# Gated feed-forward: activations in two float32r parts, weights cast to float32r in place, where activations had three bf16 parts

## The chip, the cores and the metric

One core of a Trainium2 chip runs the whole kernel. The metric is the device time of one execution in microseconds, lower is better. The engines are TensorE (PE, its weight loads apart as PEld), VectorE (DVE), ScalarE (ACT), GpSimd (POOL) and the queue of SyncE (SP), each with its own order of instructions, held together by semaphores.

## The reference

The kernel is a two-layer decoder over 8 batches of 256 tokens and 256 features, with six sublayers, each followed by a residual sum and a layer norm. The change touches the last one:

```python
wg = w_gate.astype(f32) / 127          # 768 x 256, integers from -127 to 127
wu = w_up.astype(f32) / 127            # 768 x 256
wd = w_down.astype(f32) / 127          # 256 x 768
gate = einsum('bsd,hd->bsh', x, wg)
up = einsum('bsd,hd->bsh', x, wu)
h = silu(gate) * up
x = layernorm(x + einsum('bsh,dh->bsd', h, wd))
```

Activations are float32. The weights are small integers, and so one narrow part holds each of them without loss.

## The kernel before

The sublayer before the feed-forward is a masked cross-attention over 8 batches (`attention_mask`, L1343). Its last rounds and the feed-forward overlap: on every engine the order is written out by hand.

**Tiling.** The feed-forward works on pairs of batches (PAIR = 512 token columns). A pair has HT = 6 chunks of 128 hidden features, and there are NG = 24 chunks n. `gate_up(n)` (L1473) multiplies, for each of gate and up, two blocks k of 128 features by the 512 columns, three parts each: 6 matmuls into one bank for gate (L1481 to L1488) and 6 for up. The banks alternate with n: the gate half of chunk n waits for `prod` of chunk n-2, the up half for `h_made` of n-2 (L1483). `down(t)` (L1500) makes the output of batch t: for each of 2 token tiles 6 blocks k of hidden features and 3 parts, 36 matmuls of 256 columns. There the stationary tile is a 128x128 slice of an activation part, and the moving one is `w_down`. It waits for all six `low` of its pair.

**Parts.** A float32 activation is held as three bf16 parts. For x, `split_x` (L1945, GpSimd) makes them per batch in four instructions: high copy, remainder, middle copy, low difference. Batches 0 to 4 are split during the attention (L1984), 5 to 7 between the first `low` (L1994 to L1999). For the hidden values the parts are `high` (ScalarE, L1715), `rest` (VectorE, remainder, L1834), `middle` (ScalarE, L1721) and `low` (GpSimd, L1962).

**A chunk's way.** `tanh(n)` (ScalarE, reads the gate bank), `hidden(n)` (VectorE, L1820: first half `(tanh+1)*gate`, which signals `prod`; second half times up, which signals `h_made`), `high`, `rest`, `middle`, `low`. ScalarE's order is tanh(n), middle(n-1), high(n) (L1733 to L1742), VectorE's rest(n-1), hidden(n) (L1879 to L1881). VectorE also takes the normalisation of the outputs in between: `out_begin` (L1840) after hidden of the chunks n with n % 6 of 3 and 4, `out_end` (L1867) after 5 and 0. The last batch of the attention is normalised after hidden(5) (L1887) and, on GpSimd, after low(4) (L1992, `normalise`).

**TensorE's order at the end of the attention.** gate_up(0) stands in the last round (L1579); gate_up(1) to (7) stand between the last transposes, products and projection (L1600 to L1619); from gate_up(8) on, `down` of the pair before stands behind the chunks with n % 6 of 2 and 3 (L1620 to L1628); the last two batches' products end the program (L1629 to L1643).

**Memory.** The integer weights are loaded into `dist` (L3078) and cast by `cast_weights` (L1937, GpSimd) to bf16 in `rw`. The x parts lie in `dist`, the hidden parts in `w_all_mats`, `c_feat`, `dist` and `bnd` (L1373 to L1381).

## Time and profile before

| | us |
|---|---|
| median of 3 runs | 887.89 |
| runs | 886.81 to 888.18 |
| span of the profiled execution (first to last instruction) | 885.5 |
| what lies around the span (median less span) | 2.4 |
| TensorE matmul busy in it | 847.8 (96%) |
| VectorE busy | 680.2 (77%) |
| ScalarE busy | 618.7 (70%) |
| GpSimd busy | 417.6 (47%) |

The profile gives the span of one execution; its time is that and a start and an end around it, which the 2.4 us stand for. A busy engine is one whose instructions run; a matmul's recorded length holds its way through the array too, so that the pace of matmuls is read from their starts. Times of the rows are microseconds from the span's start.

### The profile page before, as it was taken

Reading aid. Unit: us, or ns where it says so; the run is one execution under the profiler, and the core shown is the slowest. Engines: PE = TensorE matmul, PEld = TensorE weight load, DVE = VectorE, ACT = ScalarE, POOL = GpSimd, SP = SyncE. Lnnn points to the kernel's source line nnn. Section 1 sums busy time; section 2 is a strip of 40 time slices with the busy share of each in tenths; the row PEclk is TensorE's granted clock in tenths of the full one; section 3 lists DMA queues with packets and bytes.
Section 4 is the critical chain, followed back from the end, with each engine's and each line's share of the span. In section 5 each row is a group of like instructions: output and inputs, shape, how many; then the busy total and the mean of one; then the engine's idle time right before and its main releaser. Section 6 shows DMA issues by size and latency. Waiting matters only on the chain.

```text
span 885.5 us, 21124 instructions
## 1 busy us (share of the span) xinstructions
PE 847.8 (96%) x7018; PEld 613.6 (69%) x7029; DVE 680.2 (77%) x2504; ACT 618.7 (70%) x1605; POOL 417.6 (47%) x447
## 2 busy tenths in 40 slices
PE   9998999999989989999999999999999999999996
PEld 7876777777768667777676766767666766746554
DVE  4988798888997767787686766838888888866876
ACT  4547877777872578787787777748888888854441
POOL 1256546775451345435455342245445555346532
PEclk9999999999999999999999999999999999999999
DMA  9444100000005388797796877760010000000001
GB/s 323 138 119 120 46 24 26 26 25 14 14 13 215 96 279 267 228 283 229 213 283 204 269 231 231 202 210 4 28 29 28 28 29 26 2 1 1 25 24 48
DMA packets 96993, 101.89 MB, mean 115 GB/s; under 512 B 26910, under 2 KB 92190, under 8 KB 96631
## 3 DMA queue, kind: packets, MB, share of 16 engines
q1 hardware_dynamic: 96324, 100.20, 36.4%
q8 instruction: 58, 0.95, 0.4%
q14 instruction: 49, 0.39, 0.2%
q10 hardware_dynamic: 562, 0.35, 0.1%
HBM read 48.70 MB, written 51.82 MB: 114 GB/s over the span
## 4 chain that ended last, share of the span: by engine, by line
PE 46%; ACT 7%; DMA 5%; DVE 4%; issue 2%; SPq 2%; POOL 1%; DVEq 0%; ACTq 0%
PE bank L1445 6%; PE bank L223 5%; PE bank L1486 5%; PE bank L231 4%; PE bank L1429 4%; PE bank L2144 3%; PE bank L1496 3%; PE bank L1460 2%; PE bank L2130 2%; PE bank L2161 2%; ACT bias_area L2482 2%; PE bank L2194 2%; PE bank L2238 2%; PE bank L2232 1%; DMA dist<-skew_scratch 1%
## 5 line engine op out<-in xcount | busy, mean ns | idle before, releaser
L223 PE MATMUL bank<-x_feat,w_all_mats 128*128 128x256 f32 x384 | 93.2, 387 | 2.1 <-ACT q_full L341 0.6
L2879 POOL TENSOR_TENSOR bnd<-bnd,consts 128x60 f32<-128x60 f32 x64 | 18.1, 305 | 142.5 <-DMA bnd<-band_scratch 142.5
L223 PEld LDWEIGHTS bank<-x_feat,w_all_mats 128*128 128x128 f32 x384 | 70.3, 190 | 15.1 <-ACT rw L2524 3.8
L2482 ACT ACTIVATE bias_area<-bias_area,mq_two 128x256 f32<-128x256 f32 x128 | 66.4, 531 | 0.0
L1486 PE MATMUL bank<-dist,rw 128*128 128x512 bf16 x277 | 63.1, 379 | 0.6
L866 ACT ACTIVATE q_heads<-bank 128x512 f32<-128x512 f32 x64 | 37.7, 589 | 34.6 <-PE bank L682 34.6
L2658 DVE COPY q_heads<-bank 128x512 f32<-128x512 f32 x64 | 41.3, 683 | 22.4 <-PE bank L2144 22.4
L1764 DVE COPY q_heads<-bank 128x512 f32<-128x512 f32 x64 | 42.1, 685 | 19.3 <-PE bank L1445 19.2
L1651 ACT ACTIVATE Sx<-Sx,mq 128x256 f32<-128x256 f32 x128 | 54.3, 499 | 3.4 <-DVE mq L1756 3.4
L858 ACT ACTIVATE Sx<-Sx,mq 128x256 f32<-128x256 f32 x128 | 54.4, 498 | 3.0 <-DVE mq L944 3.0
L952 DVE COPY q_heads<-bank 128x512 f32<-128x512 f32 x64 | 41.9, 684 | 18.3 <-PE bank L682 18.3
L858 ACT ACTIVATE Pr<-Pr,mq 128x256 f32<-128x256 f32 x128 | 54.3, 501 | 0.9 <-DVE mq L944 0.9
L1651 ACT ACTIVATE Pr<-Pr,mq 128x256 f32<-128x256 f32 x128 | 54.4, 503 | 0.0
L1756 DVE CUSTOM_DVE_ANT_0 Sx<-bank,bias_area 128x256 f32<-128x256 f32 x128 | 46.6, 421 | 7.4 <-PE bank L1429 4.1
L2500 ACT ACTIVATE w_all_mats<-bank 108x512 f32<-108x512 f32 x32 | 19.0, 595 | 46.7 <-PE bank L2176 46.7
L1659 ACT ACTIVATE q_heads<-bank 128x512 f32<-128x512 f32 x64 | 37.7, 590 | 19.1 <-PE bank L1445 18.5
L944 DVE CUSTOM_DVE_ANT_0 Sx<-bank,bias_area 128x256 f32<-128x256 f32 x128 | 46.5, 420 | 4.7 <-PE bank L668 4.2
L1486 PEld LDWEIGHTS bank<-dist,rw 128*128 128x128 bf16 x288 | 28.2, 98 | 31.3
L231 PE MATMUL bank<-w_all_mats,aT 128*128 128x256 f32 x192 | 46.9, 387 | 1.4 <-ACT q_full L881 1.3
L2650 DVE CUSTOM_DVE_ANT_0 bias_area<-bank,dist 128x256 f32<-128x256 f32 x128 | 46.7, 421 | 1.2 <-DMA dist<-skew_scratch 1.0
L944 DVE CUSTOM_DVE_ANT_0 Pr<-bank,bias_area 128x256 f32<-128x256 f32 x128 | 46.9, 419 | 0.0
L1756 DVE CUSTOM_DVE_ANT_0 Pr<-bank,bias_area 128x256 f32<-128x256 f32 x128 | 46.5, 420 | 0.0
(288 smaller groups left out, 2451.9 us busy)
## 6 DMA issues: line engine op xcount, KB each, us to landing
dist<-skew_scratch SPq DMA_DIRECT2D x64, 296.0 KB, 4.4
skew_scratch<-rw SPq DMA_DIRECT2D x30, 588.0 KB, 4.4
bnd<-band_scratch SPq DMA_DIRECT2D x64, 108.0 KB, 2.8
band_scratch<-bias_area SPq DMA_DIRECT2D x32, 162.0 KB, 2.9
band_scratch<-bias_area SPq DMA_DIRECT2D x32, 148.0 KB, 2.6
skew_scratch<-dist SPq DMA_DIRECT2D x4, 1024.0 KB, 8.4
context_values<-dist SPq DMA_DIRECT2D x8, 512.0 KB, 2.6
v_two<-context_values SPq DMA_DIRECT2D x8, 512.0 KB, 3.5
```

Source lines behind the costliest of these rows:

```text
L223: last = pe.matmul(dst[:, m * S:(m + 1) * S], w[:, k, m * P:(m + 1) * P], rhs[:, k, :], start=(k == 0), stop=(k == FT - 1))
L231: last = pe.matmul(dst[:, t * D:(t + 1) * D], src[:, k, t * P:(t + 1) * P], w[:, k, :], start=(k == 0), stop=(k == FT - 1))
L858: last = act.activation(rows_of(g, t), rows_of(g, t), ACT.Exp, bias=mq[:, g, t:t + 1], scale=-1.0)
L944: dve.tensor_tensor_reduce(out=rows_of(g, t), in0=s_bank[g][:, t * S:(t + 1) * S], in1=bias_two[:, b % 2, t, :], scale=-1.0, scalar=3e38, ...
L952: dve.tensor_copy(PTq[:, 4 * (n % 2) + g, :, :], t_bank[g % 2][:, :].rearrange("p (k q) -> p k q", k=TT))\
L1445: last = pe.transpose(t_bank[g % 2][:, k * S + t * P:k * S + (t + 1) * P], rows_of(g, t)[:, k * P:(k + 1) * P], ident[:, :])
L1486: last = pe.matmul(dst[:, :], w_[:, k, m * P:(m + 1) * P], x_parts[i][:, k, p * PAIR:(p + 1) * PAIR], start=(k == 0 and i == 0), stop=(k = ...
L1651: last = act.activation(rows_of(g, t), rows_of(g, t), ACT.Exp, bias=mq[:, g, t:t + 1], scale=-1.0)
L1756: dve.tensor_tensor_reduce(out=rows_of(g, t), in0=s_bank[g][:, t * S:(t + 1) * S], in1=x1_bias_two[:, b % 2, t, :], scale=-1.0, scalar=3e3 ...
L1764: dve.tensor_copy(PTq[:, 4 * (n % 2) + g, :, :], t_bank[g % 2][:, :].rearrange("p (k q) -> p k q", k=TT))\
L2482: last = act.activation(rows_of(n, g)[:, t, :], rows_of(n, g)[:, t, :], ACT.Exp, bias=mq_two[:, n % 2, g, t:t + 1], scale=-1.0, accum_out= ...
L2650: dve.tensor_tensor_reduce(out=rows_of(n, g)[:, t, :], in0=s_bank[g][:, t * S:(t + 1) * S], in1=dist_pairs[:, t, 2 * j + g // 2, :, g % 2] ...
```

## The change

Activations are held in two float32r parts in place of three bf16 ones: the high one is a copy to float32r, the low one the difference, written as float32r. `rest` and `middle` go, `low` follows `high`, and `split_x` has two instructions. The weights are cast in place in `dist` from integers to float32r. Every product has 2 parts where it had 3. A part takes twice the bytes, so the areas are laid out anew by offset: weights and the even pairs' x parts in `dist`, the odd pairs' in `rw`, the high hidden parts in `w_all_mats`, the low ones in `c_feat` and, for odd pairs, in `dist` and `bnd`. The x parts now have two buffers, one for a pair each, and a split waits for the gate and up products of the pair two before. Batches 0 to 3 are split during the attention, 4 to 7 after low(6), (8), (12) and (14).

```diff
         def glu_weights():
 
-            return (dist[:, 0, 0:6, :].rearrange("p h s -> p (h s)").rearrange("p (k n) -> p k n", k=FT),
-                    dist[:, 0, 6:12, :].rearrange("p h s -> p (h s)").rearrange("p (k n) -> p k n", k=FT),
-                    dist[:, 1, 0:6, :])
-
-        dist = sb("dist", [P, TT, H, S])
+            ints = dist[:, :, :, :].rearrange("p t h s -> p (t h s)")
+            gate, up, down_ = (ints[:, i * FT * HID:(i + 1) * FT * HID] for i in range(3))
+            return (gate.rearrange("p (k n) -> p k n", k=FT), up.rearrange("p (k n) -> p k n", k=FT),
+                    down_.rearrange("p (k n) -> p k n", k=HT))
...
-            w_cells = rw[:, :, :, :, :].rearrange("p t e w v -> p (t e w v)")[:, 0:3 * FT * HID // 2].bitcast(BF16)
+            PAIR = 2 * S
+
+            def exact_cells(name, shape, at):
+
+                return nc.alloc_sbuf_tensor_at(name, shape, F32R, offset=at)
+
+            w_cells = exact_cells("glu_weight_cells", [P, 3 * FT * HID], dist_at)
             w_gate, w_up, w_down = (w_cells[:, i * FT * HID:(i + 1) * FT * HID] for i in range(3))
             w_gate, w_up = (w.rearrange("p (k n) -> p k n", k=FT) for w in (w_gate, w_up))
             w_down = w_down.rearrange("p (k n) -> p k n", k=HT)
-
-            def cells(area, pattern):
-
-                return area.rearrange(pattern).bitcast(BF16)
-
-            x_parts = [cells(a, "p h s -> p (h s)").rearrange("p (k n) -> p k n", k=FT)
-                       for a in (dist[:, 1, H // 2:H, :], dist[:, 0, 0:H // 2, :], dist[:, 0, H // 2:H, :])]
-            PAIR = 2 * S
-            h_high = cells(w_all_mats[:, 2:8, :, :], "p i k n -> p (i k n)").rearrange("p (a m t) -> p a m t", a=2, m=HT)
-            h_mid = c_feat[:, :, :].rearrange("p k n -> p (k n)")[:, 0:HT * PAIR].bitcast(BF16)\
-                .rearrange("p (a m t) -> p a m t", a=2, m=HT)
-            h_low = [cells(dist[:, 1, 0:HT, :], "p h s -> p (h s)").rearrange("p (m t) -> p m t", m=HT),
-                     bnd[:, :, :].rearrange("p t w -> p (t w)")[:, 0:HT * S].bitcast(BF16)
-                     .rearrange("p (m t) -> p m t", m=HT)]
+            x_two = [exact_cells("glu_x_even", [P, 2, FT, PAIR], dist_at + 4 * 3 * FT * HID),
+                     exact_cells("glu_x_odd", [P, 2, FT, PAIR], rw_at)]
+            h_high = [exact_cells("glu_high_even", [P, HT, PAIR], w_all_at + 4 * 2 * FT * D),
+                      exact_cells("glu_high_odd", [P, HT, PAIR], w_all_at + 4 * 8 * FT * D)]
+            low_even = exact_cells("glu_low_even", [P, HT, PAIR], c_feat_at)
+            low_odd = [exact_cells("glu_low_odd_first", [P, HT // 2, PAIR], dist_at + 4 * (3 * FT * HID + 2 * FT * PAIR)),
+                       exact_cells("glu_low_odd_last", [P, HT // 2, PAIR], bnd_at)]
...
                     if m == 0:
-                        pe.wait_ge(x_steps, 4 * 2 * (p + 1))
+                        pe.wait_ge(x_steps, 2 * 2 * (p + 1))
                     for w_, dst, done, free in ((w_gate, bank[2 * (n % 2)], g_mm, prod),
                                                 (w_up, bank[2 * (n % 2) + 1], u_mm, h_made)):
                         ge(pe, free, n - 1)
                         for k in range(FT):
-                            for i in range(3):
+                            for i in range(2):
                                 last = pe.matmul(dst[:, :], w_[:, k, m * P:(m + 1) * P],
-                                                 x_parts[i][:, k, p * PAIR:(p + 1) * PAIR],
-                                                 start=(k == 0 and i == 0), stop=(k == FT - 1 and i == 2))
+                                                 x_two[p % 2][:, i, k, :],
+                                                 start=(k == 0 and i == 0), stop=(k == FT - 1 and i == 1))
                         last.then_inc(done, 1)
 
                 def down_steps(t, tt, ks):
 
                     p, lo = t // 2, t % 2 * S + tt * P
                     for k in ks:
-                        for i in range(3):
+                        for i in range(2):
                             last = pe.matmul(down_bank(t, tt), part_of(i, HT * p + k, lo, lo + P), w_down[:, k, :],
-                                             start=(k == 0 and i == 0), stop=(k == HT - 1 and i == 2))
+                                             start=(k == 0 and i == 0), stop=(k == HT - 1 and i == 1))
                     return last
...
-                def middle(n):
-
-                    act.wait_ge(r_made, n + 1)
-                    act.activation(part_of(1, n, 0, PAIR), hid_two[n % 2], ACT.Copy).then_inc(mid_sb, 1)
...
-                    middle(n - 1)
                     high(n)
-                middle(NG - 1)
...
-                def rest(n):
-
-                    dve.wait_ge(hi_sb, n + 1)
-                    dve.tensor_tensor(hid_two[n % 2], hid_two[n % 2], part_of(0, n, 0, PAIR), ALU.subtract)\
-                        .then_inc(r_made, 1)
...
-                    rest(n - 1)
                     hidden(n)
...
-                    whole = batch(x_feat, b)
-                    high, mid, low = (batch(part, b) for part in x_parts)
+                    p, lo = b // 2, b % 2 * S
+                    high, low = (x_two[p % 2][:, part, :, lo:lo + S] for part in range(2))
                     if i == 0:
                         pool.wait_ge(xt_sb, b + 1)
                         pool.wait_ge(w_cast, 3)
-                        pool.tensor_copy(high, whole).then_inc(x_steps, 1)
-                        return
-                    pool.wait_ge(x_steps, 4 * b + i)
-                    if i == 1:
-                        pool.tensor_tensor(whole, whole, high, ALU.subtract).then_inc(x_steps, 1)
-                    if i == 2:
-                        pool.tensor_copy(mid, whole).then_inc(x_steps, 1)
-                    if i == 3:
-                        pool.tensor_tensor(low, whole, mid, ALU.subtract).then_inc(x_steps, 1)
+                        ge(pool, u_mm, HT * (p - 1))
+                        pool.tensor_copy(high, batch(x_feat, b)).then_inc(x_steps, 1)
+                    else:
+                        pool.wait_ge(x_steps, 2 * b + 1)
+                        pool.tensor_tensor(low, batch(x_feat, b), high, ALU.subtract).then_inc(x_steps, 1)
 
                 def low(n):
 
-                    pool.wait_ge(mid_sb, n + 1)
+                    pool.wait_ge(hi_sb, n + 1)
                     ge(pool, d_mm, 2 * (n // HT - 1))
-                    pool.tensor_tensor(part_of(2, n, 0, PAIR), hid_two[n % 2], part_of(1, n, 0, PAIR), ALU.subtract)\
+                    pool.tensor_tensor(part_of(1, n, 0, PAIR), hid_two[n % 2], part_of(0, n, 0, PAIR), ALU.subtract)\
                         .then_inc(lo_made, 1)
...
                     if b == 1:
                         cast_weights()
-                    if b >= 3:
-                        for i in range(4):
+                    if 3 <= b < B - 1:
+                        for i in range(2):
                             split_x(b - 3, i)
...
-                    if n in (0, 1, 2, 4):
-                        split_x(B - 3, (0, 1, 2, 4).index(n))
-                    if n in (5, 6, 7, 8):
-                        split_x(B - 2, (5, 6, 7, 8).index(n))
-                    if n in (11, 12, 13, 14):
-                        split_x(B - 1, (11, 12, 13, 14).index(n))
+                    for b, after in ((B - 4, 6), (B - 3, 8), (B - 2, 12), (B - 1, 14)):
+                        if n in (after, after + 1):
+                            split_x(b, n - after)
```

## Rows read from the trace of the kernel before

**Rows 1.** The page: granted TensorE clock, tenths of full speed, in 40 slices.
```profile
PEclk9999999999999999999999999999999999999999
```

**Rows 2.** Windows: stretch, its length; busy us (instructions) by engine; clock; DMA.
```profile
core 0: us, PE busy (x) PEld busy (x) DVE busy (x) ACT busy (x) POOL busy (x), PEclk, DMA share, GB/s
...
818.35:841.75 23.40, 23.24 (x143) 14.11 (x144) 18.76 (x34) 10.53 (x18) 11.74 (x12) 1.00 0.07 23
```

**Rows 3.** Groups by line and shape, 774.8 us on: busy us, mean ns | idle before.
```profile
L1486 PE MATMUL bank<-dist,rw 128*128 128x512 bf16 x277 | 63.1, 379 | 0.6
L1486 PEld LDWEIGHTS bank<-dist,rw 128*128 128x128 bf16 x286 | 28.0, 98 | 31.3
...
L231 PEld LDWEIGHTS bank<-w_all_mats,aT 128*128 128x128 f32 x8 | 1.5, 190 | 0.3
```

**Rows 4.** Order of time on TensorE, merged: start us, length us, engine, line.
```profile
769.96 1.04 PE L1445 MATMUL bank<-ident,Pr 128*128 128x128 f32 x8
...
796.96 1.89 PE L231 MATMUL bank<-w_all_mats,aT 128*128 128x256 f32 x8
...
818.35 13.11 PE L1486 MATMUL bank<-dist,rw 128*128 128x512 bf16 x58
831.30 0.27 PE L1496 MATMUL bank<-rw,w_all_mats 128*128 128x256 bf16 x1
...
835.23 2.75 PE L1486 MATMUL bank<-dist,rw 128*128 128x512 bf16 x11
...
841.75 13.11 PE L1486 MATMUL bank<-dist,rw 128*128 128x512 bf16 x58
```

**Rows 5.** Order of time, ScalarE and VectorE, one chunk's loop and `out_begin` behind it.
```profile
819.85 0.60 ACT L1712 ACTIVATE k_two<-bank 128x512 f32<-128x512 f32 x1 [3.82 <-PE bank L1486]
...
820.48 0.69 DVE L1824 SCALAR_TENSOR_TENSOR q_par<-k_two,bank 128x512 f32<-128x512 f32 x1 [2.57 <-ACT k_two L1712]
...
821.20 0.69 DVE L1830 SCALAR_TENSOR_TENSOR q_par<-q_par,bank 128x512 f32<-128x512 f32 x1
821.80 0.68 DVE L1847 SCALAR_TENSOR_TENSOR at<-bank,x_tok 128x512 f32<-128x512 f32 x1
821.92 0.63 ACT L1719 ACTIVATE w_all_mats<-q_par 128x512 bf16<-128x512 f32 x1 [0.96 <-DVE q_par L1830]
...
822.46 0.58 ACT L1712 ACTIVATE k_two<-bank 128x512 f32<-128x512 f32 x1
...
823.74 0.68 DVE L1837 TENSOR_TENSOR q_par<-q_par,w_all_mats 128x512 f32<-128x512 f32 x1
```

**Rows 6.** Order of time, four engines, from the attention's last product to gate_up(9).
```profile
783.51 0.38 ACT L1668 ACTIVATE w_all_mats<-bank 128x256 f32<-128x256 f32 x1 [2.54 <-PE bank L1460]
...
784.31 0.59 ACT L1712 ACTIVATE k_two<-bank 128x512 f32<-128x512 f32 x1
...
798.99 0.69 DVE L182 TENSOR_TENSOR y_sb<-bank,x_tok 128x512 f32<-128x512 f32 x1
...
801.45 1.09 POOL L1929 TENSOR_TENSOR rstd<-ve,neghalf 128x2 f32<-128x2 f32 x1 [2.03 <-DVE ve L197]
...
805.57 1.15 POOL L1960 TENSOR_TENSOR dist<-x_feat,dist 128x512 bf16<-128x512 f32 x1
...
812.05 2.54 PE L1486 MATMUL bank<-dist,rw 128*128 128x512 bf16 x11
```

**Rows 7.** GpSimd: groups by line over the span, then the order of time after the casts.
```profile
L1966 POOL TENSOR_TENSOR dist<-q_par,c_feat 128x512 bf16<-128x512 f32 x12 | 13.9, 1159 | 22.3 <-ACT c_feat L1724 22.3
...
L1952 POOL CAST dist<-x_feat 128x512 bf16<-128x512 f32 x8 | 4.9, 619 | 0.0
...
L1943 POOL CAST rw<-dist 128x1536 bf16<-128x1536 int32 x3 | 4.3, 1469 | 0.0
...
638.90 1.58 POOL L603 TENSOR_SCALAR q_par<-q_full,cols 128x512 f32<-128x512 f32 x1 [11.27 <-ACT q_full L597]
```

**Rows 8.** The chain of work that ended last, its last pieces: start us, us, what.
```profile
877.08 0.77 DVE y_sb L1852 x2
```

More of the change, by code:

```diff
@@ L18 @@
 BF16 = mybir.dt.bfloat16
+F32R = mybir.dt.float32r
 I32 = mybir.dt.int32
@@ L106, in decoder_kernel @@
         bank = [ctx.enter_context(nc.psum_tensor(f"bank{i}", [P, 512], F32)) for i in range(8)]
-        zero_cell = sb("zero_cell", [1, 1])
         x_feat = sb("x_feat", [P, FT, B * S])
         x_tok = sb("x_tok", [P, B, TT, D])
+        c_feat_at = nc.sbuf_base
         c_feat = sb("c_feat", [P, FT, B * S])
+        w_all_at = nc.sbuf_base
         w_all_mats = sb("w_all_mats", [P, len(WMATS), FT, D])
+        dist_at = nc.sbuf_base
+        dist = sb("dist", [P, TT, H, S])
+        rw_at = nc.sbuf_base
+        rw = sb("rw", [P, TT, H // FT // 2, RW, 2])
+        bnd_at = nc.sbuf_base
+        bnd = sb("bnd", [P, TT, H * NBAND])
+        zero_cell = sb("zero_cell", [1, 1])
         W = {n: w_all_mats[:, i, :, :] for i, n in enumerate(WMATS)}
@@ L235, in glu_weights @@
         def glu_weights():
-            return (dist[:, 0, 0:6, :].rearrange("p h s -> p (h s)").rearrange("p (k n) -> p k n", k=FT),
-                    dist[:, 0, 6:12, :].rearrange("p h s -> p (h s)").rearrange("p (k n) -> p k n", k=FT),
-                    dist[:, 1, 0:6, :])
-        dist = sb("dist", [P, TT, H, S])
+            ints = dist[:, :, :, :].rearrange("p t h s -> p (t h s)")
+            gate, up, down_ = (ints[:, i * FT * HID:(i + 1) * FT * HID] for i in range(3))
+            return (gate.rearrange("p (k n) -> p k n", k=FT), up.rearrange("p (k n) -> p k n", k=FT),
+                    down_.rearrange("p (k n) -> p k n", k=HT))
         ones_w = sb("ones_w", [P, P])
-        bnd = sb("bnd", [P, TT, H * NBAND])
         dist_pairs = dist[:, :, :, :].rearrange("p t h s -> p t (h s)")\
             .rearrange("p t (e s v) -> p t e s v", e=H // 2, v=2)
-        rw = sb("rw", [P, TT, H // FT // 2, RW, 2])
         rel_all = sb("rel_all", [P, NREL])
@@ L1356, in attention_mask @@
                 s_(n) for n in ("norm_steps", "normed", "y_steps", "rstd", "kept"))
-            x_steps, w_cast, g_mm, u_mm, th_sb, prod, h_made, hi_sb, r_made, mid_sb, lo_made = (
+            x_steps, w_cast, g_mm, u_mm, th_sb, prod, h_made, hi_sb, lo_made = (
                 sem(f"glu_{n}") for n in ("x_steps", "w_cast", "gate_mm", "up_mm", "tanh", "product", "hidden",
-                                          "high", "rest", "middle", "low"))
+                                          "high", "low"))
             d_mm, n_steps2, rstd2, xn_ready = (sem(f"glu_{n}") for n in ("down_mm", "n_steps", "rstd", "xn"))
@@ L1392, in part_of @@
                 p, m = divmod(n, HT)
-                if part == 2:
-                    return h_low[p % 2][:, m, lo:hi]
-                return (h_high, h_mid)[part][:, p % 2, m, lo:hi]
+                if part == 0:
+                    return h_high[p % 2][:, m, lo:hi]
+                if p % 2 == 0:
+                    return low_even[:, m, lo:hi]
+                return low_odd[2 * m // HT][:, m % (HT // 2), lo:hi]
             def down_bank(t, tt):
@@ L1896, in mask_dve @@
                         out_end(t - 1)
-                rest(NG - 1)
                 out_end(B - 3)
```

## The prediction

> **What bounds the kernel now.** I read the page first: TensorE's granted clock is at its upper level, 2.4 GHz, in all 40 slices [rows 1]. Then the windows: the gated feed-forward is the last 110 us of the span, and a pair of batches in its middle takes 23.40 us, in which TensorE is busy 23.24 [rows 2]. Then the order of time on TensorE: from one long block of gate/up matmuls (five chunks of 12, so 60; two records are missing) to the next there are 23.40 us [rows 4]. The block gives the price of a 128x512 bf16 matmul: 831.30 - 818.35 = 12.95 us over 60 = 0.2158 us. The price of a 128x256 bf16 matmul comes from the 36 of one `down`: 835.23 - 831.30 = 3.93 us, 0.109 each [rows 4]. The period follows from these two: 6 chunks x 12 x 0.2158 = 15.54 and 2 x 3.93 = 7.86, together 23.40. So TensorE alone sets the pace there, and work taken from it counts until something else comes due.
>
> What comes next is in the order of time on ScalarE and VectorE [rows 5]. A chunk goes through `tanh` (ScalarE), the two halves of `hidden` (VectorE) and `high` (ScalarE), and the next `tanh` stands behind `high` in ScalarE's order (L1734, L1742). The links, start to start: tanh to first half 820.48 - 819.85 = 0.63; to second half 0.72; to `high` 0.72; to the next tanh 0.54. That is 2.61 us a chunk, against 2.59 for a chunk's 12 matmuls. The loop is hidden now only because `down` gives it time; the change doesn't remove any link of it.
>
> **Matmuls: three parts to two.** Gate and up go from 12 matmuls a chunk to 8, `down` from 36 to 24. Over 24 chunks and 8 batches this removes 96 matmuls of 512 columns and 96 of 256: 96 x 0.2158 + 96 x 0.109 = 20.7 + 10.5 = 31.2 us of TensorE, if a float32r matmul streams a column per clock as bf16 does. No float32r matmul is in the trace. The near end is the bf16 row. The far end is one instruction of a float32 matmul, which is issued as two: 8 of 128x256 take 1.89 us; less some 0.38 for the last one's own length that leaves 7 gaps of 0.216, two clocks a column [rows 4]. I take one clock: a full product costs 4 clocks a column (two instructions of two), as four half-by-half products would, and a float32r part is such a half (two of them replace three bf16 parts). A gain below the bf16 price has no row and no reason.
>
> **Weight loads.** In gate and up the stationary tile is a weight slice, in `down` it is a 128x128 slice of the activations, now 4 bytes wide. A 2-byte load is 98 ns, a 4-byte one 190 ns [rows 3]. Under a 256-column matmul of 109 ns this could show. What speaks against it: eight transposes, each with a 128x128 float32 load and a 128-column matmul, take 1.04 us; less 0.27, the length of a short matmul as at 831.30, that is 7 gaps of 0.11 us [rows 4], so 4-byte loads follow one another at 0.11 us while matmuls run. I price `down` at 24 x 0.109 = 2.62 us; the far bound, load and stream each 0.109 and not overlapped, is 24 x 0.218 = 5.23 us a `down`. The Trainium skill ("TensorE: Matmul & The Clock Gate", section "Weight-path perf modes") speaks against the change here: it says that fast weight load is off for float32, so these loads would lose it. By its load formula (columns over 1.2 GHz) a load is 107 ns, just under the matmul, and the sum stays; the 0.11 us of the transposes agrees with that, and no row here shows a float32r load.
>
> **ScalarE and VectorE.** `middle` (24 x 0.53 on ScalarE) and `rest` (24 x 0.60 on VectorE) go. Neither was a link of the loop above, so this buys nothing directly. `high` writes 4 bytes instead of 2: 512 elements from SBUF in 630 ns as bf16, the tanh with a float32 output 585 ns [rows 5], so the price moves by -0.05 to +0.05 a link and I take none.
>
> **GpSimd.** `low` stays at 1.16 us [rows 7] and now waits for `high` directly: one link instead of three, off the loop. `split_x` goes from four instructions a batch to two (the copy of 0.62 and the difference of 1.16 [rows 7]). The float32r copy lies between 0.62 and twice that, for twice the bytes; idle time covers it. The weight casts are 1.47 us each, in place now; were they twice that, 4.4 us more end near 632 us on an engine that is needed next at 638.9 [rows 7], hidden. Batch 4 is split after `low(6)` instead of earlier; batches 6 and 7 must be split before gate_up(18). The last of these copies stands behind `low(15)`, and I find it done 0.7 us before TensorE asks: hidden, but with little cover. The wait for u_mm on the reused x buffer looks back a whole pair and is met. The moved SBUF tiles and the attention before the feed-forward I price at nothing.
>
> **The sum, walked along the queues in three stretches.** *Start to gate_up(9).* Before, gate_up(9) starts at 812.05 [rows 6]. After: tanh(1) was at 784.31, held through ScalarE's order by the last attention product [rows 6]; that product now comes earlier by what four gate/up halves lose, 0.43 each, so tanh(1) at about 782.6; four loop turns of 2.61 give tanh(5) at 793.1, its second half ends 1.95 later at 795.1. Then the last batch's normalisation, untouched: 2.3 us on VectorE and 4.1 on GpSimd (798.99 and 801.45 to 805.57 [rows 6]), 801.6; `low(5)` behind it 1.2, 802.8; down(0) 2.62. gate_up(9) at 805.5: 6.5 us earlier. In this stretch TensorE loses 9 x 0.863 + 1.31 = 9.1 us of work and gets about 3 us of new waits.
>
> *Two middle periods.* TensorE alone would need 6 x 1.726 + 2 x 2.62 = 15.6 us. The loop needs more: between the end of a second half and the next first half VectorE has 0.12 + 0.54 + 0.63 = 1.29 us; `out_end` (1.06) fits, `out_begin` (821.80 to 823.74, 1.94 [rows 5]) doesn't, by 0.65. So two chunks cost 2 x 2.61 + 0.65 = 5.87. The other four contain both `down`s: from a first half to the tanh four chunks on lie 0.72 (its product frees the bank for the gate half two chunks on), then on TensorE three gate and two up halves of 0.863 and two `down`s of 2.62, and 0.22 until ScalarE starts (a matmul's length less its pace, 0.379 - 0.216 [rows 3], and some 0.05): 0.72 + 4.32 + 5.24 + 0.22 = 10.5. With the 0.63 before it that is 11.1, against 10.4 for four bare turns. Period 17.0 instead of 23.4: 6.4 each, 12.8 for two.
>
> *gate_up(21) to the end.* Before it starts at 812.05 + 2 x 23.40 = 858.85 and the span ends at 885.5: 26.7 us. After, from gate_up(21): chunk 21, down(5) and one gate 1.73 + 2.62 + 0.86 + 0.22 = 5.4 to tanh(22); 1.35 to its second half; 0.60 + 1.94 for `out_begin` (2.5); then 0.72 and 0.72 to `high`, 0.7 to `low` (a link from ScalarE, like the 0.63), 1.2 for `low` with its signal (3.4 in all); 0.7 for the last products; 13.4. The closing VectorE chain is unchanged, 877.08 [rows 8] to 885.5 = 8.4. Together 21.8: 4.9 less. The closing `down` products that need no last part, 5.2 us, end before that chain asks.
>
> Sum: 6.5 + 12.8 + 4.9 = 24.2 us; a second walk with each engine's queue written out gives 23.5. I take 24.0: span 885.5 to 861.5. The median of the runs, 887.89, lies 2.4 above the span (runs 886.81 to 888.18), and I carry that over: 863.9.
>
> **Rivals.** *Only TensorE counts* (the loop is shorter than I read, or overlaps): the whole 31.2, 856.7. Against it: every link is a measured start-to-start time. *The 4-byte loads show in `down`*: 192 x 0.109 = 20.9 us more TensorE work, of which some 1.5 fit in its waits: 883.3. For it: the 190 ns row; against it: the transposes' pace. Partly exposed, it lies between 864 and 883. *The slower side: a float32r matmul runs at two clocks a column*, in gate_up first: TensorE work 192 x 0.432 + 192 x 0.216 = 124.4 instead of 93.5 us, 31 more less 1.8 of present waits: 917. It decides from 0.324 us a 512-column matmul on (there 8 cost as much as 12 at 0.2158). *The change doesn't do what it says*: if a float32r matmul were issued as two instructions like float32, 192 pairs would cost twice that, beyond 1000 us in all; the parts would then be pointless, and I give this the least.
>
> **Chances.** Forecast (loop-bound, 858 to 872): 0.78. TensorE only: 0.05. Loads exposed: 0.08. Two clocks: 0.07. Two instructions: 0.02. The range 857 to 876 leaves out the two slow cases and the greater part of exposed loads; its upper end takes a half-exposed pace of 0.13 (+3.3) with a longer `high` (+3) and a missed x split. A measurement of this kernel can tell about 0.2%, 1.8 us, from no change: faster 0.91, same 0.01, slower 0.08.
>
> **What would show it.** Right: 512-column float32r matmuls 0.216 us apart, 256-column ones 0.109; TensorE idle before gate_up(13), (14), released by VectorE; first-half to first-half 2.6 us in ScalarE's and VectorE's order; a period of 17 us; matmul x192 and x192. Wrong: float32r matmuls 0.43 apart; 256-column ones over 0.12; a period of 15.6 (no loop) or one in which GpSimd releases TensorE, through a late x split; or a granted clock below its upper level, as new waits of 0.5 to 2 us appear where there were almost none.

## The result and the profile after

The kernel with the change takes 864.96 us, the median of four runs (864.66 to 866.31), beside 887.35 us for the kernel before on the same chip (885.26 to 888.18): a ratio of 0.9752, interval 0.9735 to 0.9769. The forecast was 863.9. The profiled execution has a span of 862.6 us, 22.9 less than before, and the 2.4 us around it are the same.

The page of the kernel after: busy time, share and instructions by engine, then TensorE's granted clock in 40 slices, which is where it was in [rows 1].

```profile
PE 823.0 (95%) x6837; PEld 615.4 (71%) x6837; DVE 661.6 (77%) x2480; ACT 604.0 (70%) x1581; POOL 405.5 (47%) x431
...
PEclk9999999999999999999999999999999999999999
```

Windows of the kernel after: from gate_up(0) to gate_up(9), the two middle periods, and from gate_up(21) to the end.

```profile
core 0: us, PE busy (x) PEld busy (x) DVE busy (x) ACT busy (x) POOL busy (x), PEclk, DMA share, GB/s
773.70:803.95 30.25, 27.99 (x172) 21.75 (x171) 17.84 (x38) 13.59 (x26) 17.00 (x16) 1.00 0.00 1
803.95:821.92 17.97, 17.24 (x99) 14.57 (x97) 12.59 (x28) 7.42 (x13) 12.21 (x13) 1.00 0.09 30
821.92:839.90 17.98, 17.25 (x98) 14.58 (x97) 13.27 (x29) 6.82 (x12) 12.22 (x12) 1.00 0.09 31
839.90:862.60 22.70, 14.76 (x98) 13.03 (x96) 16.20 (x42) 4.09 (x7) 8.60 (x9) 0.92 0.14 47
```

The 0.92 of the last window falls behind the last matmuls: no matmul runs after 858. The middle windows answer to [rows 2]: a period of 17.98 us where there were 23.40, with TensorE busy 17.25 of it. TensorE is no longer alone: 0.73 us a period are recorded as waits. A recorded wait begins only when the last matmul's own recorded length is over, so counted from start to start more is lost: 17.98 less the 16.7 us that the matmuls of a period need at their pace. The order of time on TensorE, merged, answers to [rows 4]; the two rows from 808.54 on are the end of a `down` and the chunks 10 and 11.

```profile
803.95 2.00 PE L1494 MATMUL bank<-glu_x_odd,glu_weight_cells 128*128 128x512 f32 x8
...
808.42 0.28 PE L1504 MATMUL bank<-glu_weight_cells,glu_high_even 128*128 128x256 f32 x1
808.54 0.28 PE L1504 MATMUL bank<-glu_weight_cells,glu_low_even 128*128 128x256 f32 x1
808.66 3.82 PE L1494 MATMUL bank<-glu_x_odd,glu_weight_cells 128*128 128x512 f32 x16
812.31 1.98 PE L1494 MATMUL bank<-glu_x_even,glu_weight_cells 128*128 128x512 f32 x8
814.53 2.11 PE L1494 MATMUL bank<-glu_x_even,glu_weight_cells 128*128 128x512 f32 x8 [0.24 <-DVE q_par L1825]
817.13 2.11 PE L1494 MATMUL bank<-glu_x_even,glu_weight_cells 128*128 128x512 f32 x8 [0.49 <-DVE q_par L1825]
...
821.92 2.00 PE L1494 MATMUL bank<-glu_x_even,glu_weight_cells 128*128 128x512 f32 x8
```

Two prices come out of it. Sixteen float32r matmuls of 512 columns take 812.31 - 808.66 = 3.65 us: 0.228 each. From start to start over the whole feed-forward from 800 us on the mean is 0.229 (median 0.227), where bf16 had 0.2158. The 256-column ones start 0.119 us apart in the mean, where bf16 had 0.109. Each matmul is one instruction at nearly the bf16 pace, with 10 to 13 ns more. And VectorE's first half of `hidden` (L1825) holds TensorE ahead of gate_up(13) and gate_up(14), by 0.24 and 0.49 us.

ScalarE and VectorE in the same stretch, which answer to [rows 5]:

```profile
820.42 0.63 ACT L1727 ACTIVATE glu_high_even<-q_par 128x512 fp32r<-128x512 f32 x1 [1.48 <-DVE q_par L1831]
820.96 0.58 ACT L1720 ACTIVATE k_two<-bank 128x512 f32<-128x512 f32 x1
821.57 0.69 DVE L1825 SCALAR_TENSOR_TENSOR q_par<-k_two,bank 128x512 f32<-128x512 f32 x1 [1.18 <-ACT k_two L1720]
822.30 0.69 DVE L1831 SCALAR_TENSOR_TENSOR q_par<-q_par,bank 128x512 f32<-128x512 f32 x1
823.02 0.63 ACT L1727 ACTIVATE glu_high_even<-q_par 128x512 fp32r<-128x512 f32 x1 [1.48 <-DVE q_par L1831]
...
824.16 0.69 DVE L1825 SCALAR_TENSOR_TENSOR q_par<-k_two,bank 128x512 f32<-128x512 f32 x1 [1.18 <-ACT k_two L1720]
```

First half to first half: 824.16 - 821.57 = 2.59 us. Each of the two engines waits for the other once a turn (1.48 and 1.18 us): neither is full; their round trip is what takes the time. That is the loop that the forecast named.

The table gives the stretches of every kernel that ran, each from one profiled execution, and the time with its ratio to the kernel before on the same chip. The stretches begin at gate_up(0), so they leave out what the attention ahead of it did in that execution.

| kernel | gate_up(0) at | to gate_up(9) | two periods | gate_up(21) to end | together | time, ratio (interval) |
|---|---|---|---|---|---|---|
| before | 774.63 | 37.20 | 46.80 | 26.90 | 110.90 | 887.35 |
| after | 773.70 | 30.25 | 35.95 | 22.67 | 88.87 | 864.96, 0.9752 (0.9735 to 0.9769) |
| after_again | 776.44 | 30.26 | 35.97 | 22.67 | 88.89 | 865.73, 0.9754 (0.9740 to 0.9768) |
| e1_two_bf16 | 774.31 | 29.42 | 33.99 | 21.86 | 85.27 | 861.95, 0.9731 (0.9706 to 0.9756) |
| e2_before_no_middle | 776.77 | 35.02 | 46.80 | 26.90 | 108.72 | 886.50, 0.9989 (0.9973 to 1.0006) |
| e3_third_product | 775.77 | 36.76 | 49.91 | 28.31 | 114.97 | 892.26, 1.0063 (1.0045 to 1.0081) |
| e4_tanh_first | 777.53 | 28.33 | 36.11 | 22.98 | 87.42 | 864.85, 0.9754 (0.9730 to 0.9778) |
| e5_tanh_first_split_earlier | 777.55 | 28.35 | 35.37 | 22.98 | 86.69 | 865.13, 0.9746 (0.9730 to 0.9763) |
| e6_split_later | 775.08 | 30.27 | 42.44 | 22.68 | 95.39 | 871.14, 0.9822 (0.9797 to 0.9847) |
| e7_bf16_tanh_first_split_earlier | 775.73 | 27.29 | 33.07 | 22.02 | 82.38 | 861.60, 0.9702 (0.9687 to 0.9716) |
| e8_before_gate_two | 772.86 | 36.61 | 41.18 | 25.53 | 103.33 | 878.45, 0.9912 (0.9880 to 0.9944) |
| e9_before_down_two | 772.68 | 35.36 | 41.56 | 25.30 | 102.22 | 878.54, 0.9899 (0.9850 to 0.9947) |

Some first matmuls are missing from the traces of before, e8 and e9 (their chunks show 11 or 7 matmuls instead of 12 or 8, with a gap of one matmul ahead). Their starts are put one pace, 0.22 us, ahead of the first matmul that is recorded.

after_again is the kernel after once more, with no edit, on the same chip as e5, e6 and e7:

> The changed kernel once more, as the standard of this group of runs. 865; 30.2 us from gate_up(0) to gate_up(9), then 17.98 a period. Where its time differs from the first look, the stages ahead of the feed-forward differ, not these stretches.

Its stretches repeat within 0.02 us, but gate_up(0) comes 2.7 us later. The first column moves by up to 4.9 us between kernels, though none of the edits made for these runs touches the work ahead of it, beyond where tiles lie. So a difference of 1 or 2 us is read from the stretches, and where the times don't show it the text says so.

### The profile page after: what moved, and what is told of

Same layout as the page of the kernel before. It is cut to its first block, busy times and chain, and to the rows that moved or that the text cites. A ratio compares the mean times of both kernels' runs of the same rounds, so it can differ in the third digit from the quotient of the medians.

```text
span 862.6 us, 20687 instructions
## 1 busy us (share of the span) xinstructions
PE 823.0 (95%) x6837; PEld 615.4 (71%) x6837; DVE 661.6 (77%) x2480; ACT 604.0 (70%) x1581; POOL 405.5 (47%) x431
## 4 chain that ended last, share of the span: by engine, by line
PE 46%; ACT 9%; DVE 7%; issue 2%; DMA 1%; POOL 1%; SPq 0%; DVEq 0%; ACTq 0%
PE bank L1453 6%; PE bank L232 6%; PE bank L240 5%; PE bank L2130 4%; PE bank L1437 4%; ACT bias_area L2468 3%; PE bank L2116 3%; PE bank L1468 3%; PE bank L2147 2%; PE bank L1494 2%; PE bank L1504 2%; PE bank L2180 2%; PE bank L2224 2%; PE bank L2218 2%; DVE Sx L1757 1%
## 5 line engine op out<-in xcount | busy, mean ns | idle before, releaser
L959 DVE COPY q_heads<-bank 128x512 f32<-128x512 f32 x64 | 41.8, 683 | 18.3 <-PE bank L689 18.2
L1453 PE MATMUL bank<-ident,Sx 128*128 128x128 f32 x256 | 38.9, 282 | 5.6 <-ACT q_heads L1667 5.1
L1453 PEld LDWEIGHTS bank<-ident,Sx 128*128 128x128 f32 x256 | 27.2, 141 | 22.7 <-issue 10.8
```

Source lines behind the costliest of these rows:

```text
L959: dve.tensor_copy(PTq[:, 4 * (n % 2) + g, :, :], t_bank[g % 2][:, :].rearrange("p (k q) -> p k q", k=TT))\
L1453: last = pe.transpose(t_bank[g % 2][:, k * S + t * P:k * S + (t + 1) * P], rows_of(g, t)[:, k * P:(k + 1) * P], ident[:, :])
```

## The experiments

**Two bf16 parts in the changed order.** The same kernel with bf16 cells: the matmul count, the order on every engine and the splits are those of after. The type differs, and with it the places of the narrower areas in memory. The bits of the activations below the upper 16 are left out; the integer weights fit bf16 without loss.

```diff
-                return nc.alloc_sbuf_tensor_at(name, shape, F32R, offset=at)
+                return nc.alloc_sbuf_tensor_at(name, shape, BF16, offset=at)
...
```

> The changed kernel with every float32r cell made bf16: two bf16 parts, same order on every engine, same number of matmuls (the low bits of the activations below 16 are left out). Theory (the float32r matmul has a surcharge of 12 to 14 ns, 0.230 and 0.120 us instead of 0.216 and 0.109, and the loop tanh - hidden - high binds beside it): the pace returns to 0.216 and 0.109, but the period of a pair falls only from 17.95 to 17.0 us, held by the loop; time 862, 3 below the changed kernel. Rival 1 (only TensorE's work counts): period 15.6, time 857. Rival 2 (only the loop counts, the surcharge is hidden): period stays at 17.9, time 865.

Measured: 861.95 us, a period of 17.00. TensorE's order of time:

```profile
808.08 3.62 PE L1494 MATMUL bank<-glu_x_odd,glu_weight_cells 128*128 128x512 bf16 x16
811.53 1.89 PE L1494 MATMUL bank<-glu_x_even,glu_weight_cells 128*128 128x512 bf16 x8
813.78 1.90 PE L1494 MATMUL bank<-glu_x_even,glu_weight_cells 128*128 128x512 bf16 x8 [0.36 <-DVE q_par L1825]
816.37 1.90 PE L1494 MATMUL bank<-glu_x_even,glu_weight_cells 128*128 128x512 bf16 x8 [0.69 <-DVE q_par L1825]
```

Sixteen take 811.53 - 808.08 = 3.45 us, 0.216 each. With cheaper matmuls the waits for the loop grow from 0.24 and 0.49 to 0.36 and 0.69. The walk of the prediction, which priced float32r as bf16, is thereby tried on the kernel it really described. Its long link, from a first half over three gate halves, two up halves and two `down`s to the tanh four chunks on, can be read directly in the order of time on ScalarE and VectorE:

```profile
815.62 0.69 DVE L1825 SCALAR_TENSOR_TENSOR q_par<-k_two,bank 128x512 f32<-128x512 f32 x1 [0.54 <-ACT k_two L1720]
...
826.13 0.60 ACT L1720 ACTIVATE k_two<-bank 128x512 f32<-128x512 f32 x1 [0.67 <-PE bank L1494]
...
826.77 0.69 DVE L1825 SCALAR_TENSOR_TENSOR q_par<-k_two,bank 128x512 f32<-128x512 f32 x1
```

826.13 - 815.62 = 10.51 us where the walk had 10.5, and the period is 17.00 where it had 17.0; the last stretch is 21.86 for 21.8. The first stretch is not met: 29.42, 1.5 us less than the walk's. The type costs 88.87 - 85.27 = 3.6 us of stretches, 3.0 by the times.

**The kernel before without its middle part.** `middle` and `rest` are gone; `low` subtracts the high part and waits for that, and the second product multiplies the high cells again, so the middle part is left out of the result.

```diff
-                    middle(n - 1)
                     high(n)
-                middle(NG - 1)
...
-                    rest(n - 1)
                     hidden(n)
...
-                    pool.wait_ge(mid_sb, n + 1)
+                    pool.wait_ge(hi_sb, n + 1)
```

> The kernel before without rest and middle: low follows high, still three bf16 products, the second of them with the high part again (the middle part is left out of the result). Theory (TensorE alone sets the pace before, the two removed steps buy nothing): 887, within 1 us of the kernel before, period 23.4. Rival (ScalarE and VectorE work of 24 x 0.53 and 24 x 0.60 us was on the path): 3 us or more below before, period under 23.

Measured: 886.50 us, no difference from before that can be told, and a period of 23.40 again. But the first stretch is 35.02 us, not 37.20. The order of time on VectorE in the kernel before, ahead of the last normalisation, tells why:

```profile
787.15 1.10 DVE L1837 TENSOR_TENSOR q_par<-q_par,w_all_mats 128x512 f32<-128x512 f32 x1 [0.70 <-ACT w_all_mats L1719]
788.17 0.67 DVE L1824 SCALAR_TENSOR_TENSOR q_par<-k_two,bank 128x512 f32<-128x512 f32 x1
...
790.26 1.55 DVE L1837 TENSOR_TENSOR q_par<-q_par,w_all_mats 128x512 f32<-128x512 f32 x1
791.73 0.68 DVE L1824 SCALAR_TENSOR_TENSOR q_par<-k_two,bank 128x512 f32<-128x512 f32 x1
```

There a `rest` (L1837) takes up to 1.55 us instead of 0.69, and the next chunk's first half starts behind it. From 788.17 to 791.73 a turn takes 3.56 us. Four such turns take 12.39 us (785.05 to 797.44); in e2 the same four take 10.39 (787.07 to 797.46). All five `rest`s of this kernel that take 0.99 to 1.55 us run beside GpSimd's splitting of x (three here, two from 832.68 on); the other nineteen take 0.68 to 0.71, three of them beside a split too. In the middle periods the two operations are free, as forecast; in the first stretch they were not. The gain of 2.2 us is read from the stretches: the times, 0.7 us apart, don't show it.

**A third product put back.** The kernel after with the low part multiplied twice, in gate, up and `down`: 3 float32r matmuls where there were 3 bf16 ones, so the low part counts double in the result.

```diff
-                            for i in range(2):
+                            for c, i in enumerate((0, 1, 1)):
...
```

> The changed kernel with the low part multiplied twice: three float32r products where it has two, all else as in the changed kernel. Theory (the gain is the count of matmuls, and a float32r one costs 0.230 and 0.120): TensorE bound again, 72 x 0.230 + 72 x 0.120 = 25.2 us a period, time 892, about 4 above the kernel before by the surcharge. Rival (a good part of the gain comes from the removed steps and the lay-out): at or below the time before, 885 or less.

Measured: 892.26 us, slower than before, at a period of 24.95. One long block to the next:

```profile
825.05 8.32 PE L1494 MATMUL bank<-glu_x_even,glu_weight_cells 128*128 128x512 f32 x36
849.96 8.32 PE L1494 MATMUL bank<-glu_x_odd,glu_weight_cells 128*128 128x512 f32 x36
```

TensorE is full again: its matmuls start 0.2275 and 0.119 us apart in the mean, and 72 x 0.2275 + 72 x 0.119 = 24.95. So the float32r price stands when nothing else waits, there is no gain without the smaller number of products, and the type alone is a loss: 4.1 us against the kernel before over the stretches, although `middle` and `rest` are gone here too.

**Gate/up alone, `down` alone.** The kernel before with two of its three parts in one kind of matmul; the low part is left out of that product.

```diff
-                            for i in range(3):
+                            for i in range(2):
...
```

> The kernel before with two bf16 products in gate and up (the low part of x is left out of the result), three in down, rest and middle kept. TensorE alone: 6 x 8 x 0.2158 + 2 x 3.93 = 18.2 us a period instead of 23.40. Theory (VectorE's loop with rest in it, 2.71 us a chunk, and the loop over ScalarE come due): period 20.4, feed-forward from gate_up(0) to the end 10 us shorter, 877. Rival (only TensorE counts): period 18.2, 870.

> The kernel before with two bf16 products in down (the low part of the hidden values is left out of the result), three in gate and up. TensorE alone: 6 x 2.59 + 2 x 2.62 = 20.8 a period. Theory: the loop of 2.6 to 2.7 us a chunk is as long as a chunk's own matmuls, so TensorE still binds: period 20.8, 8.2 us shorter from gate_up(0) to the end, 879. The two gains alone, 10 and 8.2, make less than the two together would on TensorE (31), since each leaves the loop.

Measured: 878.45 and 878.54 us, periods of 20.59 and 20.78, both near what was expected. By the stretches they gain 7.6 and 8.7 us, with 20.7 and 10.5 us of matmuls removed; e8 was expected to gain 10. In e8 VectorE already holds TensorE five times, and the granted clock isn't all upper level in the first stretch. Waits of TensorE, then windows, of e8:

```profile
PE bank L1486 <- DVE q_par L1824: 4.9, 5, 1.1
...
773.00:809.70 36.70, 31.01 (x179) 17.54 (x181) 25.54 (x47) 18.68 (x35) 22.33 (x21) 0.91 0.00 1
809.70:830.30 20.60, 18.47 (x119) 11.57 (x121) 16.21 (x31) 9.71 (x17) 10.01 (x10) 1.00 0.08 26
```

e2, e8 and e9 together give 2.18 + 7.57 + 8.68 = 18.4 us, the three at once (e1) 25.6. Of the 7.2 us more, about 2 lie in the two periods: e8's own matmuls need 48 x 0.2158 + 72 x 0.109 = 18.2 us of a period that takes 20.59, because with `rest` in VectorE's turn the loop is longer (first half to first half 820.68 to 823.67, 2.99 us, where e1 has 2.59); e9's period is still all TensorE (6 x 12 x 0.2158 + 48 x 0.109 = 20.8). About 3 more lie in the first stretch (e8 had a lower clock there, so this part is rough) and 2 in the last. `rest` costs nothing while TensorE is full and something as soon as it isn't. How much of the 7.2 us is due to `rest` and `middle`, and how much to gate/up and `down` being cut together, no run separates.

**tanh(n) ahead of high(n - 1).** If the loop tanh, first half, second half, `high`, tanh binds, taking `high` out of it must help. In ScalarE's order the next tanh now comes first.

```diff
-                high(0)
                 for n in range(1, NG):
+                    if n == 5:
+                        turn_at(B - 1)
                     tanh(n)
+                    high(n - 1)
...
-                    high(n)
+                high(NG - 1)
```

> The changed kernel with ScalarE's order turned: tanh(n) before high(n-1), so that tanh no longer stands behind high. Theory (the loop binds beside TensorE): the loop is broken and the x splits come due next, period 17.9 to about 17.6, with less waiting in the first stretch: time 863.5, 1.5 below the changed kernel. Rival (TensorE's own matmuls bind, the order is without effect): 865.0.

Measured: 864.85 us, the same as after, and a period of 18.05: neither is below after, as was expected. The first stretch is 1.9 us shorter, though, and the three stretches together 1.45; the times don't show that, with gate_up(0) at 777.53. The rival's 865.0 is met in number, but not for its reason: the order does change TensorE's waits. What took the loop's place, in the order of time on TensorE and GpSimd:

```profile
815.48 5.76 PE L1494 MATMUL bank<-glu_x_even,glu_weight_cells 128*128 128x512 f32 x24 [1.09 <-POOL glu_x_even L1949]
```

```profile
812.90 1.30 POOL L1955 TENSOR_TENSOR glu_low_odd_last<-q_par,glu_high_odd 128x512 fp32r<-128x512 f32 x1 [2.86 <-ACT glu_high_odd L1727]
814.16 1.27 POOL L1949 TENSOR_TENSOR glu_x_even<-x_feat,glu_x_even 128x512 fp32r<-128x512 f32 x1
```

24 matmuls now run with no wait between chunks, so the loop is broken. But they begin 1.09 us late, behind the x split: its difference (L1949) stands in GpSimd's order behind a `low` that waited 2.86 us for its `high`, which comes later now.

**The same with the splits one chunk earlier.**

```diff
-                    for b, after in ((B - 4, 6), (B - 3, 8), (B - 2, 12), (B - 1, 14)):
+                    for b, after in ((B - 4, 5), (B - 3, 7), (B - 2, 11), (B - 1, 13)):
```

> The order of ScalarE turned as before, and every x split one chunk earlier in GpSimd's order. Theory (with the loop broken, TensorE waits 1.1 us for the x split before gate_up(12) and (18), since the split stands behind a low): these waits go, the period falls from 18.05 to 17.4, near TensorE's own 48 x 0.230 + 48 x 0.120 = 16.8; time 2.5 below the changed kernel, 862.4. Rival (another wait takes the same time, VectorE's out_begin through the bank release): period stays at 17.9 to 18.0, time 865.

Measured: a period of 17.70, between the expected 17.4 and the rival's 17.9, and stretches of 86.69 us, 2.2 less than after's. The time, 865.13 us, isn't the expected 862.4: gate_up(0) starts at 777.55 in this execution, 3.9 us later than in after's. TensorE's order of time has the wait that is left, once a period:

```profile
814.26 1.98 PE L1494 MATMUL bank<-glu_x_even,glu_weight_cells 128*128 128x512 f32 x8
816.84 4.07 PE L1494 MATMUL bank<-glu_x_even,glu_weight_cells 128*128 128x512 f32 x16 [0.60 <-DVE q_par L1825]
```

In VectorE's order `out_begin` stands between two chunks' halves, and the bank comes free that much later. So a part of what e4 was to bring is there, and the wait that is left is a link of VectorE's own queue. Whether e5 is faster than after in time is open: the intervals overlap almost wholly.

**The splits of two batches one chunk later.** The cover of the x split was put at 0.7 us; here it is taken away.

```diff
-                    for b, after in ((B - 4, 6), (B - 3, 8), (B - 2, 12), (B - 1, 14)):
+                    for b, after in ((B - 4, 6), (B - 3, 9), (B - 2, 12), (B - 1, 15)):
```

> The changed kernel with the last x split of each pair one chunk later in GpSimd's order (after low(9) and low(10), after low(15) and low(16)). Theory (the cover of the x split is about 1 us): gate_up(12) and (18) wait for GpSimd, about 1.7 us a period, period 19.7, time 868.4. Rival (the loop has enough slack to take it): 865.

Measured: 871.14 us for the expected 868.4, and a period of 21.22, 1.5 more than expected. TensorE's row with the wait, and windows around it:

```profile
816.52 1.73 PE L1494 MATMUL bank<-glu_x_even,glu_weight_cells 128*128 128x512 f32 x5 [2.65 <-POOL glu_x_even L1949]
```

```profile
813.80:816.50 2.70, 0.07 (x1) 0.00 (x0) 2.49 (x9) 0.58 (x2) 2.53 (x3) 1.00 0.00 0
816.50:819.00 2.50, 2.48 (x8) 1.94 (x9) 1.23 (x4) 1.23 (x2) 2.04 (x2) 0.70 0.31 105
819.00:821.00 2.00, 2.00 (x7) 1.57 (x6) 1.51 (x4) 0.63 (x1) 0.00 (x0) 0.53 0.00 0
821.00:824.00 3.00, 3.00 (x16) 2.51 (x15) 1.38 (x2) 1.34 (x3) 1.88 (x3) 1.00 0.25 87
```

The wait is 2.65 us, where the expectation had 1.7 for the whole effect; the split stands behind a `low` that itself waited 2.17 us for its `high`. Behind the wait the granted clock is 0.70 and then 0.53 of full, the lower of the two levels (1.2 GHz) for most of 4.5 us, and seven 512-column matmuls start 0.427 us apart instead of 0.228. The two parts can be told apart. gate_up(12) starts 11.17 us behind gate_up(9), in after 8.36: 2.8 us of the 3.2 that the period grew. From gate_up(12) to the next `down` it is 7.21 us instead of 6.76: 0.4 us is what the lower clock adds, since the rest of the slower matmuls fills the waits for the loop that after has there. So the longer wait is the greater part of what the expectation missed, and the clock the smaller.

The Trainium skill ("TensorE: Matmul & The Clock Gate", section "Why this matters for your kernels") warns that an idle gap between bursts of matmuls brings the lower clock back. These windows agree in kind, though the gap of 2.65 us is shorter than those that the page warns of.

In the kernel after the split is done in time. GpSimd's order of time, then TensorE's row of gate_up(18):

```profile
827.58 1.29 POOL L1949 TENSOR_TENSOR glu_x_odd<-x_feat,glu_x_odd 128x512 fp32r<-128x512 f32 x1
```

```profile
830.26 1.98 PE L1494 MATMUL bank<-glu_x_odd,glu_weight_cells 128*128 128x512 f32 x8
```

The split ends at 827.58 + 1.29 = 828.87; up to 830.26 that is 1.4 us of cover, twice the 0.7 forecast. TensorE itself is later than forecast, by 1 us a period.

**bf16, tanh first, splits earlier.** e1 and e5 together; what it leaves out is what e1 leaves out.

> Two bf16 parts (the low bits of the activations below 16 are left out), the order of ScalarE turned and the splits one chunk earlier. Theory: with the loop broken the cheaper matmul counts in full, TensorE's own 15.6 us a period plus some waits, 16.3: time 2.8 below the kernel with two bf16 parts alone, 859.2. Rival (VectorE, with 24 hidden and 8 normalisations, binds at 17): 862.

Measured: 861.60 us, the lowest of all, below both kernels with intervals that don't touch (0.9687 to 0.9716 beside 0.9740 to 0.9768 for after_again on the same chip). The period is 16.55, near the expected 16.3 and not the rival's 17, and the stretches sum to 82.38; the time missed the expected 859.2 by 2.4 us. The wait for `out_begin` stays, 0.54 us here, as TensorE's row shows. Beside e1 the stretches are 2.9 us shorter, the times 0.35: that the reordering pays in time on top of the type isn't settled. e7 computes less exactly than after, so it is no replacement where the bits matter.

```profile
813.24 3.87 PE L1494 MATMUL bank<-glu_x_even,glu_weight_cells 128*128 128x512 bf16 x16 [0.54 <-DVE q_par L1825]
```

## Why the prediction was right, step by step

**What bounds the kernel.** Right: TensorE alone before, and the loop next. e3 fills TensorE and loses the gain; e4 breaks the loop and its waits go.

**Matmul price: mis-sized, by 10 to 13 ns each.** Taken as bf16's 0.2158 and 0.109, measured 0.229 and 0.119. A period holds 48 and 48 of them: TensorE's own need is 48 x 0.229 + 48 x 0.119 = 16.7 us, not 15.6. In the forecast's chain of four chunks with two `down`s, five gate/up halves cost 0.92 instead of 0.863 and a `down` 2.86 instead of 2.62: 11.2 us instead of 10.5, and a period of 17.7 instead of 17.0. Measured, the chain is 11.36 (first half at 816.38, tanh at 827.74) and the period 17.98. e1 gives the other half of the proof: with bf16 prices the same chain and period are met to 0.01. So this one term explains most of the 1.95 us missing in the middle (10.85 saved, 12.8 forecast). The last stretch is 22.67 us for 21.8; as e1 has 21.86 there, the type accounts for nearly all of that too; by the prices about 0.4 of it are the matmuls on the walk's path and 0.1 the longer `low`, and the rest isn't worked out.

**Weight loads.** The rival that loads and stream don't overlap in `down` (0.218) is out at 0.119. Its mild form is not: the measured time lies at the near end of "partly exposed", 864 to 883, and 10 ns on each matmul of `down` is what a slightly exposed load would look like. Whether the loads are behind the 10 to 13 ns isn't settled. TensorE's weight loads after, grouped:

```profile
L1494 PEld LDWEIGHTS bank<-glu_x_odd,glu_weight_cells 128*128 128x128 f32 x96 | 17.6, 188 | 5.0 <-DVE q_par L1825 1.6
...
L1504 PEld LDWEIGHTS bank<-glu_weight_cells,glu_low_even 128*128 128x128 f32 x48 | 9.2, 192 | 0.1
```

A float32r load is recorded at 188 to 192 ns, the 4-byte length of [rows 3], against 98 for bf16. The section "Weight-path perf modes" of the Trainium skill's page "TensorE: Matmul & The Clock Gate" has the fast load off for float32, without saying whether float32r counts as that. The trace's longer record would agree; that such a load is what delays a 230 ns matmul no run shows. Against it stands that the float32 matmuls of this kernel, with loads of the same recorded length, keep 0.216 us an instruction; for a cost at each matmul rather than at each column stands that it changes little between 512 and 256 columns (13 and 10 ns by the means, 11 and 11 by the medians).

**ScalarE and VectorE.** `high` at 632 ns beside 630: right. `middle` and `rest` "buys nothing directly": right in the periods (e2: 23.40), wrong in the first stretch of the kernel before, where e2 alone gains 2.2 us, and as a judgement on the future: once TensorE has less to do, they would be links (e8, e9).

**GpSimd.** Groups by line, after:

```profile
L1955 POOL TENSOR_TENSOR glu_low_even<-q_par,glu_high_even 128x512 fp32r<-128x512 f32 x12 | 15.5, 1290 | 12.5 <-ACT glu_high_even L1727 12.5
...
L1926 POOL TENSOR_SCALAR x_tok<-y_sb,mv,rstd 128x256 f32<-128x256 f32 x4 | 4.9, 1223 | 0.2
...
L1922 POOL TENSOR_TENSOR rstd<-ve,neghalf 128x2 f32<-128x2 f32 x2 | 1.4, 712 | 11.7 <-DVE ve L206 11.7
L1946 POOL CAST glu_x_odd<-x_feat 128x512 fp32r<-128x512 f32 x2 | 1.2, 616 | 0.0
```

`low` takes 1.29 us with its 4-byte output, not 1.16; the copy stays at the near bound, 0.62. The last normalisation is 0.71 + 2 x 1.22 = 3.2 us, forecast 4.1: its first step took 1.09 us in [rows 6] and its other two 2.96 instead of 2.43, where a `rest` ran on VectorE beside each. e2 bears this out: the kernel before without `rest` and `middle` has 0.71 and 2.43 too, while e9, which keeps them, has 1.08 for the first step.

**The three stretches.** First: 6.95 us gained, forecast 6.5; the cheaper normalisation, 0.9 us, outweighs the dearer matmuls (e1, without the dearer ones, gains 7.8). Middle 10.85 for 12.8, last stretch 4.2 for 4.9. Together 22.0 where the sum had 24.0 (24.2 by the stretches). The prediction read the first recorded matmul at 812.05 as the start of gate_up(9); the true first one isn't in the trace, and the start is 811.83. That makes its first stretch 0.2 us too long and its last 0.2 too short, which cancels in the sum. That the span fell by 22.9 and not by 22.0 is the start of gate_up(0), 0.9 us earlier in this execution, of which nothing in the change is the known cause. So some 1 us of how near 863.9 came to 864.96 is luck: the gain of the stretches was put 2.0 too high.

**The rivals.** Only TensorE: out, as a period of 17.98 us holds 16.7 of matmuls; in e1, with the prices that this rival used, the period is 17.00 and not its 15.6. Two clocks a column, or two instructions: out by the first pair of starts.

**The signs.** Idle time ahead of gate_up(13) and (14), released by VectorE; 2.59 us from first half to first half; 192 and 192 matmuls (96 + 96, and 48 + 48 + 48 + 24 + 24): seen. A pace of 0.216, a period of 17: not with float32r, both with bf16. The 256-column matmuls, at 0.119, stay just under the 0.12 that was named as a sign of being wrong. The granted clock that might have fallen behind new waits stayed at its upper level here for as long as matmuls ran. The longest such wait, at the end of the attention, is 1.5 us:

```profile
PE bank L1477 <- DVE at L1781: 1.5, 1, 1.5
PE bank L1494 <- DVE q_par L1825: 1.5, 4, 0.5
```

## What to carry to other kernels

When work is taken from an engine that is full, write out the next loop link by link, from start to start, before counting the gain: 31.2 us of matmuls went and 22.0 came back, and the loop could be read in the old trace. A new type's matmul isn't priced until one has been seen; a surcharge of 10 to 13 ns on each of 384 was the largest error here. Operations with cover are free only as long as the cover lasts, and several cuts together can give more than each by itself (25.6 against 18.4).

## What the runs showed of the hardware

- A float32r matmul is one instruction at nearly the bf16 pace: 0.229 us for 512 columns and 0.119 for 256, beside 0.216 and 0.109 for bf16 in the same order of work (e1). Where the 10 to 13 ns come from is open.
- GpSimd's subtraction of 512 elements takes 1.29 us when it writes float32r and 1.16 when it writes bf16 [rows 7]; its copy takes 0.62 either way.
- VectorE's subtraction `rest` takes 0.69 us alone and 0.99 to 1.55 beside GpSimd's splitting of x, in the kernel before, though not beside every split; GpSimd's first step of the normalisation (128x2) takes 0.71 us without `rest` (e2) and 1.09 beside it (e9: 1.08).
- Waits of 2.65 us (e6) and 2.39 us (e8, ahead of 786.81) on TensorE were followed by the lower clock: 0.53 and 0.50 in the windows behind them. In e8 a wait of 1.59 us, the last of three within 6 us, was followed by 0.56. A wait of 1.5 us was followed by it in one execution and not in another, so the length of the wait alone doesn't decide.
- The same program reaches gate_up(0) 2.7 us apart in two executions of the kernel after. 1.1 of it arises behind such a wait of 1.5 us: the same group of TensorE starts in after and then in after_again as below, and the next group that waits for ScalarE starts at 296.17 and 298.03. The granted clock of 280 to 290 is 1.00 and 0.85. The rest is open.

```profile
286.63 1.58 PE L2376 MATMUL bank<-ident 128*128 128x128 f32 x12 [1.52 <-PEq L662]
```

```profile
287.40 2.90 PE L2376 MATMUL bank<-ident 128*128 128x128 f32 x12 [1.53 <-PEq L662]
```
